# Adding the sorted expert results to the first group's rows: from GpSimd to VectorE, in a graph-attention and mixture-of-experts kernel

## What is computed

```python
x = x + gnn(layernorm(x), in2, adj, W, b, w1, b1, w2, b2)
xf = layernorm(x)
probs = softmax(xf @ gate_w + gate_b)
top2_vals, top2_idx = top_k(probs, 2)
cw = zeros((N, 8)).at[arange(N)[:, None], top2_idx].add(top2_vals)
for e in range(8):
    h = gelu(xf @ W1[e] + b1[e], approximate=False)
    out += cw[:, e:e + 1] * (h @ W2[e] + b2[e])
return x + out
```

## Time and profile before

| what | us |
|---|---|
| three runs, median | 475.42 |
| three runs, lowest and highest | 475.42, 478.28 |
| the profiled execution, its own time | 474.09 |
| span of its trace | 472.1 |

### The profile page before, as it was taken

The page is one execution under the profiler, slowest core; times in us unless marked ns, Lnnn a source line. Parts: engine busy times, 40 slices in busy tenths (PEclk is TensorE's granted clock), DMA queues, the critical chain, the costliest instruction groups (busy, mean ns, idle before and its releaser), DMA issues.

```text
span 472.1 us, 6948 instructions
## 1 busy us (share of the span) xinstructions
PE 423.9 (90%) x2306; PEld 226.2 (48%) x2306; DVE 370.8 (79%) x844; ACT 187.3 (40%) x319; POOL 172.6 (37%) x211
## 2 busy tenths in 40 slices
PE   2699999989978999999999799998589899999995
PEld 2582444434423534445344345445357566656553
DVE  0437788799899899898999898965548677757786
ACT  1619930032310121020211121319666766667762
POOL 8920502002002202002000077777102777777491
PEclk9859999999999999999999989999999999999999
DMA  5999999999951999968900011111500333211552
GB/s 187 203 106 105 105 106 152 200 164 132 103 52 8 110 144 220 122 64 73 105 2 1 0 40 47 35 52 47 150 1 13 115 94 98 87 46 46 158 154 82
DMA packets 45428, 43.97 MB, mean 93 GB/s; under 512 B 4449, under 2 KB 41585, under 8 KB 45138
## 3 DMA queue, kind: packets, MB, share of 16 engines
q0 software_dynamic: 20928, 25.13, 44.2%
q1 hardware_dynamic: 23714, 18.39, 14.4%
q10 hardware_dynamic: 752, 0.02, 0.1%
HBM read 81.86 MB, written 11.99 MB: 199 GB/s over the span
## 4 chain that ended last, share of the span: by engine, by line
PE 52%; DVE 27%; ACT 9%; DMA 6%; issue 4%; ACTq 0%; SPq 0%; DVEq 0%
PE bank L1214 24%; DVE c L982 13%; DVE maskT L748 4%; DMA x<-in_x 4%; PE bank L1133 3%; ACT maskT L690 2%; DVE maskT L1058 2%; PE bank L1251 2%; PE bank L1327 2%; PE bank L1297 2%; ACT x L559 2%; DMA share<-in_L_gnn_inlayer 2%; PE bank L1309 2%; PE bank L1311 1%; PE bank L1310 1%
## 5 line engine op out<-in xcount | busy, mean ns | idle before, releaser
L1214 PE MATMUL bank<-c,Y 128*128 128x512 f32 x512 | 236.9, 607 | 14.0 <-DVE c L982 13.4
L982 DVE SCALAR_TENSOR_TENSOR c<-g_row,r_col,maskT 128x512 f32<-128x512 f32 x256 | 179.6, 740 | 13.4 <-PE bank L1214 11.2
L1214 PEld LDWEIGHTS bank<-c,Y 128*128 128x128 f32 x512 | 91.9, 191 | 143.0 <-DVE c L982 79.9
L511 POOL DMA_INDIRECT choice_y<-Y,mask x54 | 60.5, 1120 | 45.7 <-DVE Y L1052 30.7
L496 POOL DMA_INDIRECT sorted_x<-rows,share x40 | 45.3, 1133 | 67.3 <-DVE share L951 55.4
L444 POOL DMA_DIRECT2D mask<-in_adj x24 | 15.5, 655 | 146.0 <-DVE maskT L748 146.0
L1058 DVE SCALAR_TENSOR_TENSOR maskT<-g_row,maskT 128x1024 f16<-128x1024 f32 x24 | 32.1, 1337 | 28.9 <-ACT maskT L690 28.9
L748 DVE STREAM_TRANSPOSE maskT<-mask 128x1024 uint32<-128x1024 uint32 x32 | 39.4, 1233 | 0.0
L684 ACT ACTIVATE g_row<-bank,b1T 128x512 f32<-128x512 f32 x48 | 31.7, 686 | 18.4 <-PE bank L1311 18.2
L1327 PE MATMUL bank<-w2hl,maskT 128*128 128x128 f16 x192 | 34.0, 222 | 0.0
L1329 PE MATMUL bank<-w2hl,maskT 128*128 128x128 f16 x192 | 33.8, 221 | 0.0
(11 more groups left out here) (193 smaller groups left out, 645.4 us busy)
## 6 DMA issues: line engine op xcount, KB each, us to landing
mask<-in_adj POOLq DMA_DIRECT2D x24, 512.0 KB, 18.8
mask<-in_adj POOLq DMA_DIRECT2D x32, 128.0 KB, 25.7
mask<-sorted_x SPq DMA_DIRECT2D x27, 132.0 KB, 2.7
sorted_x<-share SPq DMA_DIRECT2D x2, 1584.0 KB, 29.1
maskT<-choice_y SPq DMA_DIRECT2D x10, 256.0 KB, 4.8
share<-in_L_gnn_inlayer SPq DMA_DIRECT2D x2, 1024.0 KB, 9.6
share<-in_x POOLq DMA_DIRECT2D x8, 256.0 KB, 11.8
out<-x SPq DMA_DIRECT2D x8, 256.0 KB
```

What stands on the lines that cost most here:

```text
L511: pool.indirect_dma_start(out=choice_y, out_offset=bass.IndirectOffsetOnAxis(ap=xt_id[:, t % XR, i, D:D + 1].bitcast(U32), axis=0), in_=y_ ...
L982: dve.scalar_tensor_tensor(c[:, k % CR].rearrange("p (s i) -> p s i", i=32), g_row[:, s * ST:s * ST + ST].rearrange("p (s i) -> p s i", i= ...
L1214: mm(bank[:, par, :], Y[:, k], c[:, k % CR], start=(k == 0), stop=(k == NK - 1)).then_inc(c_used, 1)
```

## The change

GpSimd's last loop goes. VectorE gets a function `add_choices(s)`, called at the end of the items i = 46 to 50, that is, s = 0 to 4, once in each of the last five passes of its item loop, behind `low_dense(i-1)` and `finish(i-2)`. It waits for both loads of `yin` of s, adds the first half to `x2`, waits on `first_added` for this result, and adds the second half to `x2`, which gives `out_added`. So there are again two adds of 128 x 512 floats for each of five groups, but the first now writes to `x2` instead of `yin`. Nothing else is changed: loads, stores and their order on SP, and the programs of PE and ACT stay.

```diff
@@ -530,14 +530,6 @@
             for t in range(NT):
                 place_choice(t)
 
-            for s in range(HEAD):
-
-                part = slice(s * TS, s * TS + TS)
-                pool.wait_ge(yin_in[s], 32)
-                pool.tensor_tensor(yin[:, s, 0], yin[:, s, 0], yin[:, s, 1], ALU.add).then_inc(first_added, 1)
-                pool.wait_ge(first_added, s + 1)
-                pool.tensor_tensor(x2[:, part], x2[:, part], yin[:, s, 0], ALU.add).then_inc(out_added, 1)
-
@@ -1078,6 +1070,14 @@
+            def add_choices(s):
+
+                part = slice(s * TS, s * TS + TS)
+                dve.wait_ge(yin_in[s], 32)
+                dve.tensor_tensor(x2[:, part], x2[:, part], yin[:, s, 0], ALU.add).then_inc(first_added, 1)
+                dve.wait_ge(first_added, s + 1)
+                dve.tensor_tensor(x2[:, part], x2[:, part], yin[:, s, 1], ALU.add).then_inc(out_added, 1)
+
@@ -1107,6 +1107,8 @@
                 if i > CHOOSE:
                     next(routers[2], None)
+                if i >= len(ITEMS) - HEAD:
+                    add_choices(i - len(ITEMS) + HEAD)
             low_dense(ND - 1)
             for item in ITEMS[-LAG:]:
                 finish(item)
```

## The result

Over 20 runs of each kernel the change took 477.54 us in the median against 476.03 before, 1.51 more. The ratio is 1.0028 with a 95% interval of 1.0016 to 1.0040: slower by 1.33 us (0.76 to 1.90), small, but clear of no change. The profiled execution took 475.75 us with a span of 473.7 us, against 474.09 and 472.1.

What follows compares the result with a forecast made beforehand. It took the last dense steps, paced by ACT's L690 then VectorE's L1058, as the bound. The adds' 3.13 us less 1.23 gained gave 1.90 on 475.42: 477.3 us, range 475.3 to 479.3.

Steps and rivals of the forecast that it cites:

- Sum: Whole kernel: span 1.9 us longer, 474.0 us, and a median time of 477.3 us, 0.4% more.
- Cost of one add: VectorE, last five passes: each add 0.68 us long, 0.60 us to the next instruction's start.
- Wait between the adds: VectorE's second add waits 0.07 us for the first's result, making the pair 1.35 us.
- The step: Last dense steps: VectorE needs 3.53 us against a rhythm of 3.09, so the pair sticks out by 0.44.
- The gain from GpSimd: Five steps from 446.15: without GpSimd's adds lengthening L1058 they take 15.43 us instead of 16.66, a gain of 1.23.
- The cost against no adds: Last five steps: measured from the undisturbed rhythm, VectorE's adds cost 3.13 us.
- The last pass pays in full: Before the last L1058 VectorE has no idle time, so the fifth pair, 1.35 us, lies fully on the path.
- Loads and tail: VectorE's wait for loads and the later stores of groups 4 and 6: priced at nothing, at worst a few tenths.
- Rival A: The adds fit into VectorE's idle time in each step, leaving only the gain: 474.2 us; chance 0.08.
- Rival B: DMAs, not GpSimd, lengthen L1058 in the last steps, so it stays long: 480.9 us; chance 0.04.
- Rival C: PE's clock falls while it waits for VectorE near the end: 2.0 us more at worst, 479.3 us; chance 0.06.
- Rival D: Adds late in some other way, by store order or a late load: about 478 us; chance 0.08.

Runs made afterwards that it cites:

- e2: The changed kernel with the second of VectorE's two adds per group left out; ratio 0.9983 to the kernel before.
- e1: The changed kernel with all ten adds left out; ratio 0.9972 to the kernel before.
- e5: The changed kernel with VectorE's five pairs of adds one pass earlier, in passes 45 to 49; ratio 0.9999 to the kernel before.
- e3: The changed kernel with the pair of group 4 moved behind the last L1058 and finish(49); ratio 1.0019 to the kernel before.
- e6: The kernel before, with GpSimd's pair of each group held until the L1058 of passes 45 to 49 is done; ratio 1.0053 to the kernel before.
- e8: As e3, with SP storing group 6 ahead of groups 0 to 4; ratio 0.9993 to the kernel before.

## Why the prediction was right, point by point

- *Sum.* Forecast 1.90 us, 477.3 us. Measured 1.33 (0.76 to 1.90), 477.54; in the profiled executions 1.6 in the span and 1.79 over the last passes. That the time came within 0.3 us of the forecast is in part luck: the three runs that I started from had a median of 475.42, the twenty have 476.03, so I began 0.61 too low and added 0.39 more than the medians differ by (1.51). The shift I forecast, 1.90, lies at the upper end of the measured interval.
- *Cost of one add.* 0.68 us and 0.60 to the next start, taken from an add with an fp16 result: measured 0.68 and 0.61.
- *Wait between the adds.* I took 0.07 behind the end of the first; it is 0.03 (451.31 + 0.68 to 452.02). The pair is 1.32, not 1.35, and five of them make 0.15 us. Another 0.11 is where the L1058 of pass 46 starts, 449.13 against my 449.24. Together that is the 0.26 between 466.89 and 466.63.
- *The step.* 3.53 forecast, 3.50 measured, no idle time before L1058 from pass 47 on: as foreseen. e2 shows the threshold, e1 the undisturbed rhythm.
- *The gain from GpSimd.* Forecast 1.23, e1 gives 1.16. The cost against no adds, 3.13 forecast, is 2.95.
- *The last pass pays in full.* Shown by e5: 0.98 us less for the same pairs a pass earlier, where I had 0.91.
- *Loads and tail.* No wait for the loads, the stores through in time, tail 2.72 against 2.76. That this was close I had said; e3 shows the other side, 0.84 us once three stores leave together.
- *Rival A* (covered) falls with e2 against the change: one add is covered, two are not. *Rival B* (DMAs lengthen L1058) falls with the change itself: 1.23 us in the same traffic (DMA share 1.01 from 445 to 450); e6 shows what does lengthen it. *Rival C* (PE's clock) didn't happen in the change's profile, but it is real: the profiles of e6 and e8 have it, at about 1.1 us of the last passes each. I had argued against it that PE's gaps are shorter than its rest at the end; that was no reason, since in e8 the clock fell after a gap of 1.68 us. But the change has two such gaps and e3 and e5 one each, and they kept the clock in their profiles. In how many of the change's runs it falls isn't known. *Rival D* had nothing in the change's profile.

## What to carry to other kernels

A busy share tells nothing of where work fits; the idle time of one step does. Compare the added work with the idle time that the engine has in each pass, and look separately at the passes without any: here 0.61 us was free, the next 0.6 cost 0.4 a pass, and the same pair in the last pass all of its 1.3. Before moving work from GpSimd to VectorE, see what GpSimd's instruction holds up and whether it could run beside a VectorE instruction that reads PSUM: splitting the adds and gating GpSimd's half left 0.63 us of their cost (22.66 against 22.03), nearly all of it in the last pass, and nothing once that add had moved too (22.05), while gating alone made the kernel slower.

## What the runs showed of the hardware that I had not expected

- The end of a held instruction can be computed from the other engine's row to 0.02 us: a held 128x1024 VectorE instruction ended 1.08 or 1.09 us after GpSimd's, a held 128x512 GpSimd add 1.13 or 1.14 us after VectorE's.
- GpSimd fills of 128x1024 floats, back to back for 15 us, left such VectorE instructions at 1.23 us.
- PE's granted clock went to 0.50 soon after a gap of 1.68 us in one execution (e8), and stayed at 1.00 after the same gap in e3 and e5 and after two of them in the change's profile. At 0.50 the last second layer and its way to VectorE took 3.29 us in place of 1.86.
- A wait of VectorE on its own result of 0.68 us costs 0.11 us against an independent neighbour (0.71 from start to start against 0.60).
